# One graph layer and a mixture of experts: the batch statistics of the summed messages, taken with features on partitions

## What is computed

```python
x1 = x + relu(xl + bn(agg))          # xl = layernorm(x), agg = segment_sum(gate * value, dst)
# bn(h) = (h - h.mean(0)) * rsqrt(h.var(0) + 1e-5) * g_bn + beta_bn     (over the 625 nodes)
xn = layernorm(x1)                   # per node, over its 256 features
h  = relu(xn @ W1[e] + b1[e])        # [625, 512] for each of 8 experts
out = x1 + sum_e combine[:, e] * (h @ W2[e] + b2[e])
```

## Time and profile before

| | |
|---|---|
| median of 3 runs | 841.52 us (841.14 to 841.59) |
| the profiled execution, its own time | 839.38 us |
| its span, from the first instruction to the last | 837.3 us |
| PE busy | 783.9 us (94% of the span) |
| DVE, ACT, POOL busy | 518.7, 451.9, 454.9 us |
| granted PE clock, mean over the span | 0.965 of full |

### The profile page before, as it was taken

How to read it: one execution, slowest core, us unless ns; L and a number is a source line. 1 busy time by engine, 2 the same in 40 slices (tenths; PEclk the granted TensorE clock), 3 DMA queues, 4 the chain that set the end, 5 groups by cost and what they waited for, 6 DMA issues and landing times. The chain is left out here.

```text
span 837.3 us, 14474 instructions
## 1 busy us (share of the span) xinstructions
PE 783.9 (94%) x4536; PEld 677.4 (81%) x4537; DVE 518.7 (62%) x885; ACT 451.9 (54%) x796; POOL 454.9 (54%) x390
## 2 busy tenths in 40 slices
PE   4789999999999999999999989999999963999998
PEld 3567888888888888888888878888888852999998
DVE  3357656565656666666565377778778846556564
ACT  2434454455454445555454477776766751747570
POOL 1477777777777777777776055554544553100000
PEclk9899999999999999999999989999999975899999
DMA  6889999999999999999999756665655612003101
GB/s 176 226 256 332 356 331 342 338 337 322 334 332 334 343 339 335 337 335 334 336 327 372 270 194 222 233 221 205 241 201 200 226 30 85 1 27 101 50 25 32
DMA packets 67754, 201.73 MB, mean 241 GB/s; under 512 B 10912, under 2 KB 18878, under 8 KB 67726
## 3 DMA queue, kind: packets, MB, share of 16 engines
q1 hardware_dynamic: 41614, 118.38, 40.2%
q0 software_dynamic: 25024, 81.94, 29.3%
q10 hardware_dynamic: 1088, 1.05, 0.5%
HBM read 156.19 MB, written 45.14 MB: 240 GB/s over the span
## 5 line engine op out<-in xcount | busy, mean ns | idle before, releaser
L122 POOL DMA_INDIRECT pre<-table_dst,idx x157 | 174.0, 1108 | 50.0 <-issue 47.5
L434 POOL DMA_INDIRECT from_src<-table_src,idx x157 | 154.7, 985 | 50.7 <-issue 46.9
L354 POOL TENSOR_TENSOR hvT_lo<-hv,hvT_hi 128x1024 fp32r<-128x1024 f32 x40 | 100.2, 2508 | 114.2 <-ACT hvT_hi L349 114.2
L565 PE MATMUL p_h<-eaT_hi,w_hi 128*128 128x512 f32 (+1 forms) x320 | 136.0, 425 | 1.5 <-DVE eaT_lo L490 1.5
L514 DVE TENSOR_TENSOR pre<-pre,from_src 128x512 f32<-128x512 f32 (+1 forms) x157 | 99.5, 694 | 49.0 <-DMA from_src<-table_src,idx 48.9
L565 PE MATMUL p_h<-eaT_lo,w_hi 128*128 128x512 f32 (+1 forms) x320 | 126.1, 394 | 0.0
L565 PE MATMUL p_h<-eaT_hi,w_lo 128*128 128x512 f32 (+1 forms) x320 | 125.2, 391 | 0.0
L528 DVE TENSOR_TENSOR h_lo<-h_full,h_hi 128x512 fp32r<-128x512 f32 (+1 forms) x80 | 54.4, 680 | 96.1 <-ACT h_full L469 96.0
L574 PEld LDWEIGHTS p_h<-ident,pre 128*128 128x128 f32 x628 | 77.4, 140 | 26.0 <-DVE pre L514 5.5
L574 PE MATMUL p_h<-ident,pre 128*128 128x128 f32 x628 | 94.2, 273 | 3.9 <-DVE pre L514 3.8
L468 ACT ACTIVATE h_hi<-p_h 128x512 fp32r<-128x512 f32 (+1 forms) x80 | 47.1, 588 | 91.4 <-PE p_h L574 91.4
(11 more groups left out here) (204 smaller groups left out, 1706.8 us busy)
## 6 DMA issues: line engine op xcount, KB each, us to landing
h_val<-hv_st SPq DMA_DIRECT2D x40, 512.0 KB, 4.6
z_gate<-zg_st SPq DMA_DIRECT2D x40, 512.0 KB, 7.8
hv<-h_val SPq DMA_DIRECT2D x40, 512.0 KB, 4.4
gate<-z_gate SPq DMA_DIRECT2D x40, 512.0 KB, 3.3
ea<-in_edge_attr_dram SPq DMA_DIRECT2D x39, 512.0 KB, 7.1
raw<-in_L_ffn_W_dram SPq DMA_DIRECT2D x16, 512.0 KB, 4.7
pre<-table_dst,idx POOLq DMA_INDIRECT x157, 6.3
from_src<-table_src,idx POOLq DMA_INDIRECT x157, 6.7
```

The costliest lines, as they stand in the source:

```text
L122: pool.indirect_dma_start(pre[b][0:n, t, :], None, table_dst, bass.IndirectOffsetOnAxis(ap=idx[b][0:n, t:t + 1], axis=0)).then_inc(got_dst ...
L354: nc.gpsimd.tensor_tensor(hvT_hl[b % 2][1][:], hv[b][:], hvT_hl[b % 2][0][:], ALU.subtract).then_inc(hv_lo, 1)
L434: pool.indirect_dma_start(from_src[b][0:n, t, :], None, table_src, bass.IndirectOffsetOnAxis(ap=idx[b][0:n, T + t:T + t + 1], axis=0)).the ...
L565: nc.tensor.matmul(p_h1[c][:, 0:w], w1_hl[wp][:, k, c * P:(c + 1) * P], eaT_hl[b % 2][dp][:, k, 0:w], start=n == 0, stop=False)
```

## The change

`agg` is transposed by PE (10 transposes, features to partitions) into PSUM. There DVE takes mean and variance of each feature with `bn_stats` over 500 and 125 nodes and `bn_aggr`, for each of the two groups of 128 features. Scale and shift are now columns of 128 partitions x 2, computed from `g_bn` and `beta_bn`, which two more loads of block 1 bring into `vecs`. To bring them back to node-major rows, PE transposes each column, read 125 times over by a broadcast. That is done into `p_scale` and `p_shift` for DVE and a second time into `p_st`, which ACT copies to SBUF (`st_rows`) for POOL. The normalised sum is `agg * scale + (xln + shift)`: DVE does tiles 0 to 2, save that POOL adds the shift to tile 2; POOL does tiles 3 and 4.

The rest is done in two parts, tiles 0 to 2 and tiles 3 and 4: layer norm, transposes' copies and low parts. The first product of the first expert takes all four pieces of the first half of the nodes and then all four of the second (`parts(..., halves_first=True)`); its start waits for three tiles of `xnT_lo`, its second half for all five. PE's own transposes of the five tiles of `xln` all stand ahead of it, as before. The five small loads that are left of the seven are issued at the end of SP's list in block 3. The bias table `b1T` is copied by ACT in place of DVE. Semaphore names, the removed lines of DVE's part and lines that are only indented otherwise are left out here.

```diff
-        vecs = sb(whole, "vecs", [P, 4, KF])
+        vecs = sb(whole, "vecs", [P, 6, KF])
...
-                    for n, v in enumerate((g_int, beta_int, b2f, b2m)):
+                    for n, v in enumerate((g_int, beta_int, b2f, b2m, g_bn, beta_bn)):
                         sp.dma_start(vecs[:, n, :], column(v), allow_slow_non_contiguous=True).then_inc(v_in, 16)
...
+                    for n, v in enumerate((bg, bias)):
+                        sp.dma_start(gate_b[:, n, :], spread(v, NE)).then_inc(n_in, 16)
+                    sp.dma_start(wg_sb[:], Wg.rearrange("(k p) e -> p k e", p=P)).then_inc(n_in, 16)
+                    sp.dma_start(b1_sb[:], b1.rearrange("e (m p) -> (e m) p", p=P)).then_inc(n_in, 16)
+                    sp.dma_start(b2_sb[:], b2).then_inc(n_in, 16)
...
-                    dve.wait_ge(v_in, 64)
+                    dve.wait_ge(v_in, 96)
...
-            p_sum, p_var = p_h[0][0:TP, 0:F], p_h[1][0:TP, 0:F]
+            p_aggT = [[p_h[k][:, 0:4 * TP], p_h[2][:, k * TP:(k + 1) * TP]] for k in range(KF)]
+            p_scale, p_shift, p_st = p_h[3][0:TP, 0:F], p_b[0:TP, 0:F], p_a[0:TP, 0:2 * F]
             p_xnT = [bank[:, 0:KF * TP].rearrange("p (k n) -> p k n", k=KF)
-                     for bank in (p_h[2], p_h[3], p_y01[0], p_y01[1], p_b)]
+                     for bank in (p_h[0], p_h[1], p_h[2], p_b, p_y01[0])]
+            p_b1T = p_y01[1][:, 0:NE * KH]
...
+            def parts(pieces, halves_first=False):
+
+                if halves_first:
+                    return [(q * KH + m, m, lo, up) for q, (lo, up) in enumerate(HALF) for m in pieces]
+                return [(2 * m + q, m, lo, up) for m in pieces for q, (lo, up) in enumerate(HALF)]
...
-                    for n, v in enumerate((g_bn, beta_bn)):
-                        sp.dma_start(bn_rows[:, n, :], spread(v, F)).then_inc(n_in, 16)
...
-                    pool.wait_ge(n_in, 16 * 7)
-                    for t in range(NT):
-                        nc.gpsimd.tensor_tensor(xln[:, t, :], xln[:, t, :], bn_rows[:, 1, :],
-                                                ALU.add).then_inc(pre_add, 1)
                     nc.gpsimd.iota(expert_id[:], pattern=[[0, NT], [1, NE]], base=0, channel_multiplier=0,
                                    allow_small_or_imprecise_dtypes=True).then_inc(ids2_ok, 1)
-                    pool.wait_ge(dev_ok, NT)
-                    pool.wait_ge(sq_ok, NT)
-                    pool.wait_ge(pre_add, NT)
-                    pool.wait_ge(rs_ok, 1)
+                    pool.wait_ge(st_copied, 1)
+                    nc.gpsimd.tensor_tensor(xln[:, ND - 1, :], xln[:, ND - 1, :], st_rows[:, 1, :],
+                                            ALU.add).then_inc(pool_norm, 1)
                     for t in range(ND, NT):
-                        nc.gpsimd.tensor_tensor(dev[:, t, :], dev[:, t, :], rs[:], ALU.mult).then_inc(norm_ok, 1)
-                    for t in range(ND, NT):
-                        pool.wait_ge(norm_ok, t - ND + 1)
-                        nc.gpsimd.tensor_tensor(dev[:, t, :], dev[:, t, :], xln[:, t, :], ALU.add).then_inc(norm_ok, 1)
+                        n = 1 + 3 * (t - ND)
+                        nc.gpsimd.tensor_tensor(dev[:, t, :], agg[:, t, :], st_rows[:, 0, :],
+                                                ALU.mult).then_inc(pool_norm, 1)
+                        nc.gpsimd.tensor_tensor(xln[:, t, :], xln[:, t, :], st_rows[:, 1, :],
+                                                ALU.add).then_inc(pool_norm, 1)
+                        pool.wait_ge(pool_norm, n + 2)
+                        nc.gpsimd.tensor_tensor(dev[:, t, :], dev[:, t, :], xln[:, t, :],
+                                                ALU.add).then_inc(pool_norm, 1)
...
-                    for t in range(NT):
-                        act.wait_ge(dev_ok, t + 1)
-                        nc.scalar.activation(sq[:, t, :], dev[:, t, :], ACT.Square).then_inc(sq_ok, 1)
-                    act.wait_ge(chain2, 1)
-                    nc.scalar.activation(rs[:], rs[:], ACT.Sqrt).then_inc(std3_ok, 1)
-                    act.wait_ge(std4_ok, 1)
-                    nc.scalar.activation(ln_std[:], ln_std[:], ACT.Sqrt).then_inc(std4_ok, 1)
+                    act.wait_ge(var_ok, 1)
+                    nc.scalar.activation(bn_col[:, 1, :], bn_col[:, 0, :], ACT.Sqrt).then_inc(std3_ok, 1)
+                    act.wait_ge(b1_psum, 1)
+                    nc.scalar.copy(b1T[:], p_b1T).then_inc(b1T_ok, 1)
                     act.wait_ge(pad_ok, 2)
                     nc.scalar.copy(xnT_hl[0][:, :, N:NPAD], xnT[:, :, N:NPAD]).then_inc(pad_ok, 1)
+                    act.wait_ge(st_psum, 3)
+                    nc.scalar.copy(st_rows[:].rearrange("p a f -> p (a f)"), p_st).then_inc(st_copied, 1)
+                    for n, (lo, up) in enumerate(((0, ND), (ND, NT))):
+                        act.wait_ge(eps_ok, n + 1)
+                        nc.scalar.activation(ln_std[:, lo:up], ln_std[:, lo:up], ACT.Sqrt).then_inc(std4_ok, 1)
+                        for t in range(lo, up):
+                            act.wait_ge(xnT_psum, t + 1)
+                            nc.scalar.copy(xnT_hl[0][:, :, t * TP:(t + 1) * TP], p_xnT[t]).then_inc(xnT_hi, 1)
...
+                    for k in range(KF):
+                        dve.wait_ge(aggT_psum, k + 1)
+                        nc.vector.bn_stats(bn_st[:, k, 0:6], p_aggT[k][0]).then_inc(bn_done, 1)
+                    for k in range(KF):
+                        dve.wait_ge(aggT_psum, 2 * KF)
+                        nc.vector.bn_stats(bn_st[:, k, 6:12], p_aggT[k][1]).then_inc(bn_done, 1)
+                    for k in range(KF):
+                        dve.wait_ge(bn_done, KF + k + 1)
+                        nc.vector.bn_aggr(bn_mv[:, k, :], bn_st[:, k, :]).then_inc(bn_done, 1)
+                    dve.wait_ge(bn_done, 3 * KF)
+                    nc.vector.tensor_scalar(bn_col[:, 0, :], bn_mv[:, :, 1], EPS, None, ALU.add).then_inc(var_ok, 1)
+                    then(nc.vector.reciprocal(bn_col[:, 2, :], bn_col[:, 1, :]))
+                    nc.vector.tensor_tensor(bn_col[:, 2, :], bn_col[:, 2, :], vecs[:, 4, :],
+                                            ALU.mult).then_inc(scale_ok, 1)
+                    dve.wait_ge(scale_ok, 1)
+                    then(nc.vector.tensor_tensor(bn_col[:, 3, :], bn_mv[:, :, 0], bn_col[:, 2, :], ALU.mult))
+                    nc.vector.tensor_tensor(bn_col[:, 4, :], vecs[:, 5, :], bn_col[:, 3, :],
+                                            ALU.subtract).then_inc(shift_ok, 1)
+
+                    def normalize_sum(t):
+
+                    def ln_statistics(lo, up):
+                        for t in range(lo, up):
+                            dve.wait_ge(x1_ok, t + 1)
+                            nc.vector.bn_stats(ln_stats[:, t, :], x_sb[:, t, :]).then_inc(ln_done, 1)
+                        for t in range(lo, up):
+                            dve.wait_ge(ln_done, lo + t + 1)
+                            nc.vector.bn_aggr(ln_mv[:, t, :], ln_stats[:, t, :]).then_inc(ln_done, 1)
+                        dve.wait_ge(ln_done, 2 * up)
+                        nc.vector.tensor_scalar(ln_std[:, lo:up], ln_mv[:, lo:up, 1], EPS, None,
+                                                ALU.add).then_inc(eps_ok, 1)
+
+                    def ln_apply(lo, up, half):
+                        dve.wait_ge(std4_ok, half + 1)
+                        then(nc.vector.reciprocal(ln_std[:, lo:up], ln_std[:, lo:up]))
+                        for t in range(lo, up):
+                            nc.vector.tensor_scalar(xln[:, t, :], x_sb[:, t, :], ln_mv[:, t, 0:1], ln_std[:, t:t + 1],
+                                                    ALU.subtract, ALU.mult).then_inc(xn_ok, 1)
+
+                    def ln_lo(lo, up):
+                        for t in range(lo, up):
+                            dve.wait_ge(xnT_hi, t + 1)
+                            nc.vector.tensor_tensor(xnT_hl[1][:, :, t * TP:(t + 1) * TP], p_xnT[t],
+                                                    xnT_hl[0][:, :, t * TP:(t + 1) * TP],
+                                                    ALU.subtract).then_inc(xnT_lo, 1)
+
+                    dve.wait_ge(st_psum, 1)
+                    for t in range(ND):
+                        nc.vector.tensor_tensor(dev[:, t, :], agg[:, t, :], p_scale, ALU.mult).then_inc(scaled, 1)
+                    dve.wait_ge(st_psum, 2)
+                    for t in range(ND - 1):
+                        nc.vector.tensor_tensor(xln[:, t, :], xln[:, t, :], p_shift,
+                                                ALU.add).then_inc(shifted, 1)
+                    for t in range(ND):
+                        dve.wait_ge(scaled, t + 1)
+                        if t < ND - 1:
+                            dve.wait_ge(shifted, t + 1)
+                        else:
+                            dve.wait_ge(pool_norm, 1)
```

(65 more changed lines are left out.)

133 lines of the change are left out of this document (34 added, 99 removed).

## The result

The kernel after takes 830.66 us (median of 4 runs, 830.01 to 831.03); before, in the same measurement, 841.33 (4 runs, 840.15 to 841.59). The ratio is 0.9873, 95% interval 0.9851 to 0.9894: 1.3% faster. The predicted median was 831.9, the range 829.0 to 835.0.

A forecast was written before the change was run, and what follows sets the result against it. It took the 28.45 us from block 4's start to the first product as the bound: 10.8 saved, 1.15 lost, 9.65 gained. 839.38 - 9.65 = 829.7 profiled; with 2.14 added, median 831.9, range 829.0 to 835.0.

The forecast's parts named there:

- First part: Block 4's start to a usable scale: 4.8 us against 15.6, 10.8 us saved.
- Second part: Usable scale to the first product's start: 13.95 us against 12.8, 1.15 us lost.
- rival 1: POOL and DVE slow each other, tile 4's relu waits for POOL: gain about 7, 834.5 us; chance 0.13.
- PE's list: All five tiles' transposes stand ahead of the first product, which so waits 2.8 us for tile 4's xln.
- The clock: First product starts at a low granted clock and stays at 9.2 us; removing the sums by ones costs nothing.
- rival 2: Clock rises sooner in first product, drop in second is shorter: up to 2.3 + 1.6 us more, about 829; chance 0.07.
- SP's lists: Two more loads in block 1 delay block 2 by up to 1.0 us, costed at nothing; block 3 has room.
- The cover: POOL's and PE's existing waits in block 2 hide its later start; without them it costs 1.0 us.
- a sign of being wrong: Block 2's first product of gathered rows coming later than 49.83 would show the prediction wrong.
- The median: Median of the runs lies 2.14 us above the profiled execution, added to 829.7 to give 831.9.

The follow-up runs named there:

- e3: Kernel after with DVE doing all five tiles, POOL's operations, ACT's copy and the second spreading removed: same time, first product 0.3 us sooner.
- e2: Kernel after with PE's transposes of tiles 3 and 4 moved behind two pieces of the first product: median 828.81 us.
- e7: Kernel after with late transposes of tiles 3 and 4, g_bn and beta_bn columns loaded in block 3, 20 unused matmuls before the first product: median 826.12 us.
- e9: Against e7: 24 unused matmuls for 20, four more behind the transposes of tiles 0 to 2, late transposes one piece later: median 826.74 us.
- e4: Kernel after with the g_bn and beta_bn columns loaded at the end of SP's list in block 3 instead of block 1: ratio 0.9878 to before.
- e6: Kernel after with layer norm, copies and low parts of all five tiles in one part, order of product pieces kept: median 831.39 us.
- e8: Kernel after with the five small loads issued ahead of block 4's weights again: 0.3 us later to the first product.
- e1: Kernel before with only its seven small loads moved to the end of SP's list in block 3: median 3.9 us below before's.
- e5: Kernel after with unused matmuls on PE, 20 behind the scale's spreading, 10 behind the transposes of tiles 0 to 2: block 4 1.95 us shorter.

## Why the prediction held

Its working was right in the steps, and the profiled time came out at 830.01 for a forecast of 829.7.

- **First part.** 5.0 us to a usable scale for 4.8 predicted; `bn_stats` over 500 columns out of PSUM 0.69 (0.68), the two over 125 columns 0.39 (0.4), the spreading 0.80 (0.68).
- **Second part.** 14.2 us for 13.95. Of DVE's three joins and three relus the first ran alone, at 0.33, and the other five took 0.86 to 0.88 beside POOL, for 0.9; `bn_stats` was undisturbed. One row has about the size of the excess of 0.25: the epsilon of the second part (L1074), 0.48 for some 0.2 predicted.
- **POOL and rival 1.** POOL was done 1.5 us before DVE's last relus, as the sum had it. What the sum didn't see is that POOL's share is worth nothing (e3): it never priced DVE doing all five tiles, which takes about as long as what DVE lost beside POOL. The Trainium skill (GPSIMD Engine Reference, section 1, Specifications) names the contention for instructions with two SBUF inputs; by it the joins and relus are slow, and what has one operand in SBUF is not. The trace agrees: beside POOL the three `bn_stats` took 1.06, and three low parts, with one operand from PSUM and POOL at work from 699.99 on, 1.11 on the chain.
- **PE's list.** The product did wait for tile 4's transposes, and e2 priced that at 3.0 (2.8 predicted). The prediction named them as lost by the order of that list. But with the order alone (e2) only 0.15 of them were left at the end of its profile: 1.3 went into the first product, 1.55 into the second. In e7 and e9, with PE kept busy as well, 2.85 and 3.5 us reached the end. That the unused matmuls kept the second product's clock up there is not shown, since after, e3, e4 and e6 have it up without them.
- **The clock.** The first product stayed at 9.16 for 9.2 at 0.50 to 1.00, as costed, though e4 and e6, with the same matmuls, had 8.74 and 7.93: its length is partly chance. The second, costed as unchanged, gained 1.50. That is the second half of rival 2, and it isn't the statistics' doing: e2 and e8 have the same new statistics and take 8.59 and 8.58 there. In before, e1, e2 and e8 the clock fell within 0.5 us of that product's start, behind the 20 small matmuls of the routing; in the other seven, with the same 20 ahead of it, it did not fall. In these four the small matmuls began 4.3 to 4.6 us behind the clock's rise in the first product, in after, e3, e4, e6 and e7 4.9 to 6.4 us behind it; in e5 and e9 the clock was up before that product. No run tested this order, so what decides the fall was not settled, and the 1.50 is luck as far as is known.
- **SP's lists.** The later start of block 2 was bounded by 1.0. It was 2.75: the two loads took 2.06 of it, since one issue lasted 1.52 for the 0.5 costed, and the rest stood ahead of them. The cover held for most of it: block 2's first product of gathered rows came at 50.15, later than 49.83 and so a sign of being wrong, but by 0.3 us, which can't be told from chance (e4). Whether the 1.19 us by which block 4 started later belong to the change was not shown: it starts at 683.36 to 685.14 in the five profiles with four loads in block 1 and at 683.46 (e2) to 688.05 in the six with six.
- **The median.** The prediction added 2.14 us for the distance of the profiled execution to the median. Here that distance is 0.65. So 1.49 too much was added there, while the working came out 0.3 too low; together this is the miss of 1.2 us (831.9 against 830.66). Either distance is that of the one execution that was profiled, so this part of the miss is chance.

So the terms that carried the sum were right, and two that weren't in it, +1.19 and -1.50, nearly cancelled in the profiled execution; that is luck. The gain in front of the first product has two sources: the small loads that PE waited for (4 us in the old kernel, by e1; e8 points to the two spread ones, `g_bn` and `beta_bn`, as what made that wait long, but no run moved these two alone), and the shorter chain of statistics (the other 5, by difference). The two parts of the layer norm (e6) and POOL's share (e3) add nothing that can be measured. The order of the first product's halves and ACT's copy of `b1T` were not tested by themselves.

## What to carry over

- Where PE is idle ahead of dense work, count a start moved forward only with the clock at which the work will run: dense work in the gap shortened the product from 9.16 to 7.25 (e5), and of 3.0 us of earlier start 1.7 were left at the product's end without it (e2).
- Before a distance in one profile is put down to an edit, look at the clock of the stages behind it: e6's end is 3.0 us nearer than after's, 2.7 of it by the clock of two products that the edit doesn't touch.
- A wait for small loads can be a wait for the large ones ahead of them on the queue; removing those can be worth as much as moving the wait (5.11 us to land with them ahead, 2.48 without; e1, e8).
- Before an operation on two SBUF tensors is shared with POOL, compare with DVE doing it alone: at 0.33 a piece alone against 0.87 beside POOL the help was worth nothing (e3).

## What the runs showed of the hardware

- By the granted clock, it rose from 0.50 4.3 us into the dense first product in after, 6.2 us into it in e2, 1.5 in e6; the same product took 7.93 to 10.48. In e7 the clock was 1.00 across a stop of PE of 1.58 us and fell to 0.50 behind a second one of 1.21, just ahead of the product; in e9, with stops of 0.91 and 0.28 there, it stayed at 1.00.

```profile
699.73 0.63 PE L1273 MATMUL p_h<-xnT_hi,w1e_hi 128*128 128x314 f32 x1 [1.21 <-DVE xnT_lo L1090]
```
```profile
699.78 0.41 PE L1274 MATMUL p_h<-xnT_hi,w1e_hi 128*128 128x314 f32 x1 [0.28 <-DVE xnT_lo L1090]
```

- It rose within the unused dense matmuls in e5, e7 and e9, 2.9 to 4.3 us behind the first of them. The first stage of after, with 29 instructions of PE, all transposes, has 0.50 in all of its 19.20 us. The Trainium skill (TensorE: Matmul & The Clock Gate, Part 4) says that transposes don't engage the full clock. No run here shows it by itself: PE was busy for only 6.88 of the 19.20 us, and in the kernel before the dense sums by ones stayed at 0.50 for their 4.63 us, too:

```profile
683.68 4.63 PE L1186 MATMUL p_h<-agg,ones 125*125 125x256 f32 x10 [1.74 <-DVE ones L1029]
```

- In the six kernels that issue six small element-wise column loads in one list, the first four took SP 0.39 to 0.55 us each to issue and the fifth 0.54 to 1.52 (1.52 in after); in e5 it was the sixth that was slow, at 1.04.
